# One core, a Mamba and FFN block: the last projection accumulated in the token layout, its scale folded into the weights, all orders laid out anew

## The reference

```
x = x + attention(condition(x, delta_t, ...))
x = x + ffn(cond2(x, expert_ids, ...))
```

```
def _tlin(x, w, s):
    return jnp.einsum('bsi,oi->bso', x, w) * s
h = jax.nn.silu(_tlin(x, w1_w, w1_s)) * _tlin(x, w2_w, w2_s)
h = jax.nn.gelu(_tlin(h, h1_w, h1_s), approximate=False)
h = jax.nn.gelu(_tlin(h, h2_w, h2_s), approximate=False)
return _tlin(h, w3_w, w3_s)
```

## Time and profile before

| | us |
|---|---|
| median of three runs | 1011.33 (1011.26 to 1012.2) |
| the profiled execution | 1006.92 |
| its span, first to last instruction | 1005.1 |
| busy: PE, DVE, ACT, POOL | 913.3, 901.2, 794.8, 849.9 |
| mean granted TensorE clock | 0.973 |

### The profile page before, as it was taken

How to read it: one execution, slowest core, us unless ns; L and a number is a source line. 1 busy time by engine, 2 the same in 40 slices (tenths; PEclk the granted TensorE clock), 3 DMA queues, 4 the chain that set the end, 5 groups by cost and what they waited for, 6 DMA issues and landing times.

```text
span 1005.1 us, 13837 instructions
## 1 busy us (share of the span) xinstructions
PE 913.3 (91%) x4368; PEld 596.3 (59%) x4368; DVE 901.2 (90%) x696; ACT 794.8 (79%) x1294; POOL 849.9 (85%) x427
## 2 busy tenths in 40 slices
PE   4798777879989999999989999999989998999998
PEld 3555455756755566555755666556756585557556
DVE  2898999999999999999999999999999999998700
ACT  6968866898789976998599977898689968888632
POOL 0697998899999998999989898999999999778300
PEclk9798889889999999999999999999999999999999
DMA  3866765546636755556545836566465666545100
GB/s 111 280 207 210 208 183 148 160 151 211 207 121 190 211 160 176 174 172 190 174 139 171 252 118 197 162 194 177 159 198 151 205 178 180 171 151 137 63 1 16
DMA packets 97671, 167.44 MB, mean 167 GB/s; under 512 B 9920, under 2 KB 33408, under 8 KB 97344
## 3 DMA queue, kind: packets, MB, share of 16 engines
q1 hardware_dynamic: 97600, 166.57, 55.0%
HBM read 159.19 MB, written 7.34 MB: 166 GB/s over the span
## 4 chain that ended last, share of the span: by engine, by line
PE 30%; DVE 29%; issue 19%; ACT 12%; POOL 8%; DMA 2%; DVEq 0%; POOLq 0%; ACTq 0%; SPq 0%
DVE bank_d L1025 21%; PE bank_y L1322 7%; PE bank_m L1151 5%; POOL state L637 4%; ACT L668 4%; DVE state L1023 4%; PE bank_m L1235 3%; PE bank_m L1228 3%; DVE state L1030 3%; ACT bank_d L796 3%; POOL state L642 2%; PE bank_m L1242 2%; DMA c_rows<-bc_store 1%; PE bank_m L1201 1%; PE bank_m L1217 1%
## 5 line engine op out<-in xcount | busy, mean ns | idle before, releaser
L637 POOL TENSOR_TENSOR state<-du,b_rows 128x1024 f32<-128x1024 f32 (+1 forms) x288 | 616.6, 2166 | 46.9 <-PE bank_y L1322 43.7
L1025 DVE TENSOR_TENSOR_SCAN bank_d<-bank_d,state 128x1024 f32<-128x1024 f32 (+1 forms) x225 | 460.9, 2048 | 15.3 <-ACT bank_d L796 14.5
L796 ACT ACTIVATE bank_d<-delta,a_neg 128x512 f32<-128x512 f32 (+1 forms) x540 | 323.1, 634 | 79.0 <-DVE state L1030 73.6
L1322 PEld LDWEIGHTS bank_y<-ident,state 128*128 128x128 f32 x2048 | 240.9, 145 | 80.9 <-issue 62.4
L1322 PE MATMUL bank_y<-ident,state 128*128 128x128 f32 x2048 | 264.3, 280 | 17.1 <-DVE gated L1041 12.2
L1030 DVE TENSOR_TENSOR state<-bank_d,c_rows 128x1024 f32<-128x1024 f32 (+1 forms) x225 | 248.2, 1103 | 6.4
L642 POOL TENSOR_TENSOR state<-state,c_rows 128x1024 f32<-128x1024 f32 (+1 forms) x63 | 133.5, 2119 | 12.2 <-DVE state L1023 11.4
L1151 PE MATMUL bank_m<-xnT,w_conv 128*128 128x508 f32 (+7 forms) x288 | 117.8, 556 | 2.1 <-DVE x1T L1050 1.0
L1235 PE MATMUL bank_m<-hidA,h_s 128*128 128x512 f32 (+1 forms) x256 | 110.7, 581 | 6.6 <-ACT hidA L868 6.4
L1228 PE MATMUL bank_m<-hidB,h_s 128*128 128x512 f32 (+1 forms) x256 | 107.4, 567 | 1.9 <-DVE hidB L1064 1.0
L1023 DVE TENSOR_TENSOR_SCAN state<-bank_d,state 128x1024 f32<-128x1024 f32 (+1 forms) x45 | 91.9, 2041 | 0.0
(11 more groups left out here) (149 smaller groups left out, 1020.1 us busy)
## 6 DMA issues: line engine op xcount, KB each, us to landing
b_rows<-bc_store SPq DMA_DIRECT2D x256, 256.0 KB, 5.0
c_rows<-bc_store SPq DMA_DIRECT2D x256, 256.0 KB, 4.7
wsel<-merged SPq DMA_DIRECT2D x32, 512.0 KB, 3.4
merged<-hidA SPq DMA_DIRECT2D x8, 512.0 KB, 3.1
h_s<-in_h SPq DMA_DIRECT2D x2, 1024.0 KB, 9.6
xin<-in_x SPq DMA_DIRECT2D x7, 256.0 KB, 4.1
out<-cT SPq DMA_DIRECT2D x7, 256.0 KB, 3.8
wsel<-in_factors SPq DMA_DIRECT2D x8, 160.0 KB, 3.4
```

Source lines behind the costliest of these rows:

```text
L637: nc.gpsimd.tensor_tensor(split(unit_state(u)), du[:, d, :, :width(g)], per_half(b_rows, u), ALU.mult).then_inc(S.bx_ready, 1)
L796: ins = act.activation(split(unit_decay(u))[:, h], delta[:, d, h, :width(g)], ACT.Exp, scale=a_neg[:, h, n:n + 1])
L1025: dve.tensor_tensor_scan(decay, decay, drive, 0.0, ALU.mult, ALU.add).then_inc(S.scanned, 1)
L1322: ins = pe.matmul(bank_y[:, h, s * P:(s + 1) * P], split(unit_state(u))[:, h, s * LEN:(s + 1) * LEN], ident[:, :], start=(n == 0 and s == ...
```

## The change

The fill `w3` and its take on DVE are gone. `fill_tok` computes the projection in the layout with tokens on the partitions: for each sequence the hidden tile is the stationary operand and the weights move (128 columns), the four chunks are accumulated, and the residual `x1T` is transposed on top into the same PSUM region. Because the scale lies along the free axis in this layout, it is multiplied into the weights once, on DVE, with a row that one more DMA broadcasts to all partitions. The column `w3_s` leaves `col`. All tables are new; those lines that the text speaks of are below, the other entries change in the same way.

```diff
-FILL = {"norm": (-44.5, -25, -30, -27, -27, -26.5, -26),
+FILL = {"norm": (-46, -24.5, -33, -26.5, -26, -25.5, -27.5),
-        "ur0": (-11.5, -21, -25, -24, -20, -23.5, -19.5),
+        "ur0": (-9.5, -19, -20.5, -25, -20.5, -24, -19.5),
-        "z0": (-7.5, -16, -26.5, -23.5, -20, -18.5, -16),
-        "z1": (-21.5, -16, -21.5, -18, -23, -18.5, -19),
-        "dbc0": (-28, -10.5, -10, -10, -10, -10, -9.5),
+        "z0": (-38.5, -24, -26.5, -24.5, -18.5, -24.5, -23),
+        "z1": (-39, -17, -27, -18.5, -23.5, -20, -27),
+        "dbc0": (-39, -10, -10, -10, -10.5, -10.5, -10.5),
-        "dt01": (-21, -9.5, -8, -8, -9.5, -9.5, -7.5),
+        "dt01": (-33.5, -9, -8.5, -8.5, -9.5, -9.5, -9.5),
-        "dt10": (-0.5, -2, -3, -0.5, -1, -1, -2),
-        "dt11": (3, 0.5, -1, -0.5, -1, -1, -5.5),
+        "dt10": (8, -1.5, -2, -0.5, -1, -0.5, -5),
+        "dt11": (3.5, -1, -5.5, -0.5, -0.5, -0.5, -7.5),
-        "w3": (71.5, 71.5, 71.5, 71, 70, 77.5, 83.5),
-        "tok": (73, 73, 72.5, 73.5, 71, 88.5, 95.5)}
+        "tok": (74.5, 72.5, 72.5, 71, 71.5, 94.5, 86.5)}
-SETUP = {"fuse": -12.5, "wi0": -12.5, "wo0": 4.5, "wi1": -12, "wo1": 9.5, "wi2": 10, "wo2": 11, "wi3": 18.5,
+SETUP = {"fuse": -27.5, "wi0": 1.5, "wo0": 4.5, "wi1": -9, "wo1": 9.5, "wi2": 11, "wo2": 13, "wi3": 17.5,
-MERGE_LAG = 2
+MERGE_LAG, W3_AT = 2, 20.0
-          "gelu": ((63, 61.5, 61.5, 61.5, 61, 74, 120), (71.5, 69.5, 71, 69.5, 71.5, 110, 148.5)),
+          "gelu": ((61.5, 61.5, 62, 61.5, 60, 68.5, 134), (74, 69.5, 70, 70, 72, 95.5, 100)),
-       "x1": (43, 44, 44.5, 44, 43, 44, 48),
+       "x1": (42, 44.5, 44, 44, 43.5, 44.5, 58),
-       "w3": (74, 74, 74, 73, 74.5, 86, 95.5),
-       "aggr": (-18.5, -34.5, -38, -33, -32.5, -32.5, -30)}
+       "aggr": (-33.5, -29, -34.5, -30, -32.5, -34, -32.5)}
...
-                                 (h2_s[:, :, :], h2), (w3_s[:, :, :], w3)):
+                                 (h2_s[:, :, :], h2), (w3_s[:, :, :], w3),
+                                 (w3_scale[:, :], w3_row.to_broadcast([P, HID]))):
                     sp.dma_start(dst, src).then_inc(S.back_w_loaded, 16)
...
                 if 0 < g < NG - 1:
-                    wait_filled(dve, g - 1, "w3")
+                    wait_filled(dve, g - 1, "tok")
...
-            def take_w3(g):
-                w = width(g)
-                x1T = rooms(g)[3]
-                wait_filled(dve, g, "w3")
-                dve.scalar_tensor_tensor(x1T[:, :w], bank(g, "w3"), c("w3_s"), x1T[:, :w],
-                                         ALU.mult, ALU.add).then_inc(taken_of(g, "w3"), 1)
+            def scale_w3():
+                dve.wait_ge(S.back_w_loaded, 7 * 16)
+                dve.tensor_tensor(w3_s[:, :, :], w3_s[:, :, :], w3_scale[:, :].unsqueeze(1).to_broadcast([P, FC, HID]), ALU.mult).then_inc(S.w3_scaled, 1)
...
-            def fill_w3(g):
-                hidB = rooms(g)[5]
+            def fill_tok(g):
+                x1T, hidB = rooms(g)[3], rooms(g)[5]
+                wait_taken(pe, g, "res")
+                wait(pe, S.w3_scaled, 1)
                 wait_hidden(pe, g, "h2_")
-                for q in range(FC):
-                    ins = pe.matmul(bank(g, "w3"), w3_s[:, q], hidB[:, q, :width(g)], start=(q == 0), stop=(q == FC - 1))
-                return ins
-
-            def fill_tok(g):
-                x1T = rooms(g)[3]
-                wait_taken(pe, g, "w3")
                 for s in range(sequences(g)):
-                    ins = pe.transpose(bank(g, "tok")[:, s * P:(s + 1) * P], x1T[:, s * LEN:(s + 1) * LEN], ident[:, :])
+                    at = slice(s * LEN, (s + 1) * LEN)
+                    for q in range(FC):
+                        pe.matmul(bank(g, "tok")[:, at], hidB[:, q, at], w3_s[:, q], start=(s == 0 and q == 0), stop=False, skip_group_check=True)
+                    ins = pe.matmul(bank(g, "tok")[:, at], x1T[:, at], ident[:, :], start=False, stop=True, is_transpose=True, skip_group_check=True)
                 return ins
```

More of the change, by code:

```diff
@@ L37 @@
                   ("a_log", HALVES * NST), ("ln_g", 1), ("ln_b", 1), ("reduce_b", 1), ("glu_b", 2),
-                  ("w1_s", FC), ("w2_s", FC), ("h1_s", FC), ("h2_s", FC), ("w3_s", 1),
+                  ("w1_s", FC), ("w2_s", FC), ("h1_s", FC), ("h2_s", FC),
                   ("delta_t", BATCH // 2), ("freq", 1), ("amp", 1)):
@@ new lines @@
+SETUP = {"fuse": -27.5, "wi0": 1.5, "wo0": 4.5, "wi1": -9, "wo1": 9.5, "wi2": 11, "wo2": 13, "wi3": 17.5,
+         "wo3": 17.5, "wi4": 18.5, "wo4": 19.5, "wi5": 22.5, "wo5": 25, "wi6": 27, "wo6": 29, "wi7": 34,
+         "wo7": 33}
+MERGE_LAG, W3_AT = 2, 20.0
+TAKE_LAG = {"norm": (8, -1.5, -47.5, -156, -30.5, -37.5, -75.5),
[12 rows of a table added]
+            "out": (3, -68, 0, 1, 1.5, 2.5, 1),
[18 rows of a table added]
+            "tok": (-113.5, -92, -67.5, 1.5, -15.5, -52.5, -109.5)}
+ACT_AT = {"scale": (-43.5, -41.5, -41.5, -36.5, -36.5, -41, -41),
+          "normalise": (-38.5, -27.5, -32.5, -28.5, -27.5, -28.5, -29),
+          "softplus": ((-37, -5, -5, -6.5, -6.5, -6, -8.5), (6.5, 5, 2, 1.5, 1.5, 2, -1.5)),
+          "copied": ((19, 17.5, 18.5, 18.5, 18.5, 17.5, 19), (34, 35, 34, 33, 33, 33.5, 49.5)),
+          "front": (0, -12.5, -10, -10, -11, -11, -11.5),
+          "silu": (51.5, 51.5, 53.5, 52.5, 51, 53, 26),
+          "skip": ((8.5, 4, 5, 12, 9.5, 8.5, 17), (29.5, 5, 28, 28, 23, 29.5, 22.5)),
+          "sigmoid": (41, 40.5, 41.5, 41.5, 42, 43, 57),
+          "gelu": ((61.5, 61.5, 62, 61.5, 60, 68.5, 134), (74, 69.5, 70, 70, 72, 95.5, 100)),
+          "power": (-39, -28.5, -34, -29, -31, -29.5, -32.5)}
@@ new lines @@
+DECAY_LEAD = 2
+VEC = {"gated": ((20, 20, 20.5, 21.5, 21.5, 19, 20.5), (35.5, 36, 36, 36, 36, 37, 38)),
[5 rows of a table added]
+       "stats": (-40, -36.5, -37.5, -33, -33.5, -34, -34),
+       "aggr": (-33.5, -29, -34.5, -30, -32.5, -34, -32.5)}
+GPS = {"residual": (-26, -10.5, -9.5, -13, -14.5, -13.5, 38.5),
+       "delta": ((-22, -4, -4, -5, -4.5, -5, -6.5), (6.5, 7.5, 2, 9, 10, 3, 1.5)),
+       "inputs": ((-20.5, -4, -4, -3.5, -4.5, -3.5, -6.5), (10.5, 9.5, 12, 10.5, 11, 7.5, 2.5)),
+       "mix": (-34, -36, -38.5, -36, -36, -38, -35.5)}
@@ L179 @@
 DIRECT = {"gate": NG - 1, "h1_": NG - 1, "h2_": NG - 2}
-BY_VECTOR = ("glu0", "res", "up0", "up1", "up2", "up3", "w3")
+BY_VECTOR = ("glu0", "res", "up0", "up1", "up2", "up3")
 def fill_plan():
@@ L227, in build @@
 def build(nc, x, expert_ids, columns, conv_rows, w_in, w_x, w_dt, w_out, w_reduce, w_glu,
-          wi, wo, factors, w1, w2, h1, h2, w3, merged, bc_store, out):
+          wi, wo, factors, w1, w2, h1, h2, w3, w3_row, merged, bc_store, out):
     PI = float(np.pi)
@@ L249, in build @@
         w3_s = sb("w3_s", [P, FC, HID])
+        w3_scale = sb("w3_scale", [P, HID])
         ident = sb("ident", [P, P])
@@ L1113, in _ @@
                             take_up(g, f)
-                    if rel == slot(VEC, g, "w3"):
-                        take_w3(g)
                 if at == SETUP["fuse"] + MERGE_LAG:
                     take_fused()
+                if at == W3_AT:
+                    scale_w3()
                 for e in range(EXPERTS):
@@ L1181, in fill_glu @@
             def fill_glu(g, m):
-                wait(pe, S.back_w_loaded, 6 * 16)
+                wait(pe, S.back_w_loaded, 7 * 16)
                 gy = rooms(g)[0]
@@ L1376 @@
         host(ffn + "w1_s").reshape(FC, P).T, host(ffn + "w2_s").reshape(FC, P).T, host(ffn + "h1_s").reshape(FC, P).T,
-        host(ffn + "h2_s").reshape(FC, P).T, host(ffn + "w3_s").reshape(P, 1),
+        host(ffn + "h2_s").reshape(FC, P).T,
         np.repeat(host("condB_deltat").reshape(BATCH // 2, 2).T, P // 2, axis=0),
@@ L1393 @@
         "h2": chunked(host(ffn + "h2_w").T), "w3": chunked(host(ffn + "w3_w").T),
+        "w3_row": host(ffn + "w3_s").reshape(1, HID),
     }
```

40 lines of the change are left out of this document (9 added, 31 removed), and 120 rows, old and new, of tables (FILL, TAKE_LAG, VEC).

## The result

The changed kernel takes 1000.13 us in the median of six runs (998.47 to 1000.73); before, run beside it, takes 1009.0 (1005.35 to 1012.2, six runs). The ratio is 0.9894, 95% interval 0.9868 to 0.9919. The profiled executions differ by 8.45 us (1006.92 and 998.47, span 996.6). No execution of before lies near its median here: three took 1005.35 to 1006.73 us and three 1011.26 to 1012.2.

The account below looks back on a forecast made before the run. DVE was taken to bound the middle and PE the last stretch. Takes -4.36, product +0.61, start -0.8, end -0.4 and other orders 0 sum to -4.95 us: 1011.33 becomes 1006.4 us, range 1001.0 to 1012.0.

Parts of the forecast that it names:

- DVE bounds the middle: Between first scan and last product, DVE has under 1 us of slack per group, so work leaving its queue shortens the run.
- the takes are worth their spacing: Seven w3 takes leave DVE's middle stretch, each priced by its start-to-start time: 6 x 0.66 + 0.40 = 4.36 us gone.
- The scaling product: One added DVE product of w3_s with the broadcast row, in group 0: 0.61 us, between 0.5 and 1.2.
- 0.124 us a pass and 4.4 us a stage: PE's merged stage, 32 passes of 128 columns: +0.5 us per full group, into 6 us of slack.
- The rival of exposed loads: PE's weight loads not hidden, 4.8 us more per full group: slower, 1013 us and up, say 1017; chance 0.04.
- my sign of being wrong: The prediction is wrong if passes of PE's merged stage come over 0.2 us apart.
- The start: Group 0's new order lets scan 4 start near 39.6 instead of 40.42 us: -0.8 us, between -2 and +1.5.
- The end: Behind the last product: a 0.65 us wait for w3's take goes, wo to h1 grows 0.25: -0.4 us.
- one of my signs of being wrong: The prediction is wrong if the stretch behind DVE's last product grows.
- 0 for the other orders: In the middle, the remaining table changes get 0 us, as no row gives a sign; left to the range.
- the constant 4.4 us: Before's median, 1011.33, lies 4.4 us above its profiled execution, 1006.92; the forecast difference is taken from the median.
- stalls go too: Rival: the new order also removes up to half of DVE's 21.8 us of waits: 996 to 1003, say 1000.5; chance 0.12.

Follow-up runs that it names:

- fold_late: fold_w3place with ACT taking the merged stage's bank 2.5 units behind its fill in groups 0 to 6; 1013.23 us, ratio 1.0026.
- fold_old: The merged computation in the tables of before, with the merged stage at tok's old place; 1017.76 us, ratio 1.0070.
- new_first60: fold_old with the pieces whose old place lies ahead of unit 60 at their new places; 1015.44 us, ratio 1.0051.
- w3place_first60: fold_w3place with the pieces before unit 60 at their new places; 1033.08 us, ratio 1.0225.
- late_first60: fold_late with the pieces ahead of unit 60 at their new places; 1007.52 us, ratio 0.9967 against before.
- fold_w3place: The merged computation in the tables of before, with the merged stage and its take where w3's fill was; 1040.25 us, ratio 1.0272.
- early_take: The changed kernel with ACT taking the merged stage's bank at its fill where possible (groups 3, 4, 5: 1.5 units sooner); 1014.58 us.
- after_same: The changed kernel measured again, unaltered, beside before; 1000.21 us, ratio 0.9906.
- before_res: The kernel before with POOL's residual product of groups 3 to 5 three units later, its place in the changed kernel; 1011.72 us.

## Why the prediction was right or wrong

**Right in kind, 0.8 us too large: DVE bounds the middle, and the takes are worth their spacing.** Forecast -4.36, rows -3.5. I read the price off the one take that stands between a product and a scan; the five between a scan and its product cost 0.52 and not 0.66. The scaling product: 0.61 forecast, 0.59 measured. In the old order it took 1.77 us (fold_late, at 72.06), and in the new order of the first 60 units 0.68, so its price depends on its place too.

**Right: PE.** Forecast 0.124 us a pass and 4.4 us a stage; measured 0.111 and 4.1. No load shows. The rival of exposed loads is out. Passes came about 0.2 us apart, my sign of being wrong, in stages of fold_old and new_first60 alone, where the granted clock was down (0.52 to 0.76).

**The start**: forecast -0.8, and the scans of units 10, 16 and 24 of group 0 start 1.12, 1.09 and 1.02 us sooner. The parts were off by more, in both directions. Scan 4 started here:

```profile
38.54 1.23 DVE L1025 TENSOR_TENSOR_SCAN bank_d<-bank_d,state 128x512 f32<-128x512 f32 x1 [0.25 <-ACT bank_d L796]
```

The forecast was 39.6, and before it was 40.42. Scan 0 started at 30.43 and not at 31.25: ACT's additional `ur0` take did not delay it. Against that, scan 9 waited 1.26 us for its decay, more than I had counted.

**The end**: -0.4 forecast, +0.05 measured. It was one of my signs of being wrong that this stretch grows, though 0.05 us is next to nothing. The wait for the take of `w3` went: from the last group's last projection to the end 5.7 us became 4.9, -0.76 (forecast -0.65). From the last DVE product to the last group's h1 35.9 us became 36.6, +0.74 (forecast +0.25).

**Wrong, and the step that failed: "0 for the other orders".** I wrote that "in the middle both tables give nearly the same sequences", and looked at a few places in full groups. Of the 8.45 us between the profiles the takes, the product, the start and the end make 4.0; the other 4.4 are this term, and 4.0 of them are there when group 3 begins. This is the scan of unit 24 of group 1, before and after:

```profile
188.24 2.29 DVE L1025 TENSOR_TENSOR_SCAN bank_d<-bank_d,state 128x1024 f32<-128x1024 f32 x1
182.20 2.30 DVE L1025 TENSOR_TENSOR_SCAN bank_d<-bank_d,state 128x1024 f32<-128x1024 f32 x1
```

It already starts 6.04 us sooner, when no take of `w3` has yet been due (the first is in group 2), where my terms for the start and the product give 0.2. By unit 0 of group 2 DVE's waits were 9.1 us before and 4.1 after (on ACT 5.7 and 2.3), and the scan of unit 8 of group 1 took 2.64 us and not 4.09 (that of group 2 then took 4.06 and not 2.40). new_first60, w3place_first60 and late_first60 put 2 to 7 us on these pieces, in three different surroundings. The views had it: groups 0 and 1 held 9.1 of the 21.8 us of waits behind the earlier trace rows, and I followed only those before scan 10.

**Wrong: "Two takers of w3's bank go too, but banks were not what DVE waited for".** True of before, and no help: with the merged computation in the old order the banks' turns and ACT's queue are what DVE waits for. fold_old, fold_w3place and fold_late are 6.4, 28.5 and 2.0 us above before. Two places cost the whole saving and more when they are wrong: the stage close ahead of `glu0` (fold_old), and its take at its own fill (fold_w3place, early_take). The changed tables avoid both in groups 3 to 5 (fill at 71, take at 72.5, `glu0` two units on), and I read over it. That the two places are enough is not shown: fold_late has both and is still above before.

**Wrong in kind: the constant 4.4 us.** I took before's median (1011.33) to be its profile (1006.92) plus something that stays. Most of it is probably the long scan, which that profile lacks and no profile of the changed kernel in its own tables has. Medians therefore differ by more than profiles (11.1 us beside each other in after_same's comparison, 8.45 in the profiles). That this scan makes the two clusters rests on three profiles of before and before_res (2.52 us at 1006.92; 7.17 and 5.97 at 1012.4 and 1012.7) and on POOL's rows. No run switched it off cleanly, and the falls of TensorE's clock add 2.2 us in one of these profiles, so it is likely and not shown.

**The account.** fold_late 1013.2, with the first 60 units new 1007.5, with the rest and the stage's own place new 1000.2. Of the last 7.3 us the profiles give 3.4 to the scan of unit 17 in group 2 (5.66 and 2.28 us). Which pieces give the other 4 was not tried, and neither was which of the first 60 units' pieces give the 5.7. The rival "stalls go too" (996 to 1003) is the case that came, but DVE's waits fell by 3.6 us only, and part of the cause, the scans beside POOL, was in none of my cases.

## What to carry to other kernels

When a step is merged into another in a hand-written order, look at both ends of the new step: what is queued behind its fill on PE, and what is queued behind its take on the engine that takes it. A take placed at its own fill cost 3.6 to 4.9 us a group here, and the saving was 0.5 to 0.7. When all orders change at once, go through the waits of the stretches with the most of them, the first groups, before giving the rest a zero. And compare the profiled execution with the spread of the times: where they lie in two clusters, look for the instruction that differs before taking differences from a median.

## What was not expected of the hardware

A scan of 128 x 1024 with both inputs in SBUF took 2.28 us at its shortest and up to 7.41 beside POOL's products; a product of POOL that takes 2.35 us otherwise took 4.36 beside such a scan. Of the scans that read PSUM none took over 2.30 us in any profile. A 512-column product on SBUF took 0.68 or 1.77 us, one of 448 columns 0.60 or 2.70. The scan of unit 17 took 2.52 and 7.17 us in two executions of the same program.

TensorE's granted clock was 0.60 in the 4 us from 628 to 632, behind a standstill of 2.02 us, and stayed at 1.00 behind one of 2.03 us at the same place of another execution of the same program.
